# Local attention over spans of 64 keys, with tiles of 32 queries on TensorE

## The reference, cut to what matters

```
def local_attention(q, k, v):
    ...
    bk2, bv2 = (look(bk), look(bv))
    ...
    mask = (it < jb) | (it > jb + w) | (jb == -1)
    sim = jnp.einsum('bhwie,bhwje->bhwij', bq, bk2) * QK_SCALE
    sim = jnp.where(mask, -jnp.finfo(sim.dtype).max, sim)
    attn = jax.nn.softmax(sim, -1)
    out = jnp.einsum('bhwij,bhwje->bhwie', attn, bv2)
```

## Time and profile before

| what | us |
|---|---|
| median of three runs | 1869.86 |
| the profiled execution | 1866.89 |
| its span, first to last instruction | 1865.1 |
| TensorE busy, 14256 matmuls | 1740.2 (93%) |
| VectorE busy | 1612.1 (86%) |
| ScalarE busy | 1560.1 (84%) |
| GpSimd busy | 1334.2 (72%) |

### The profile page before, as it was taken

One profiled execution on the slowest core, in us unless ns is written; L12 is line 12 of the kernel. 1 busy time (PEld: TensorE's weight loads), 2 busy tenths in 40 slices (PEclk: granted clock), 3 DMA queues, 4 the chain that ended last, 5 costly groups with the idle time before them and its releaser, 6 DMA issues.

```text
span 1865.1 us, 39680 instructions
## 1 busy us (share of the span) xinstructions
PE 1740.2 (93%) x14256; PEld 1364.5 (73%) x14256; DVE 1612.1 (86%) x3044; ACT 1560.1 (84%) x4889; POOL 1334.2 (72%) x1864
## 2 busy tenths in 40 slices
PE   6589999899999999999999999999999999999995
PEld 4367777677777777777777777777777777777774
DVE  5689898898998988988989989989899889899872
ACT  3289889889898898898898898988988988988882
POOL 3378777787776777877877868777777778777660
PEclk9599999999999999999999999999999999999998
DMA  3000010000010000000000001000001000000000
GB/s 112 2 1 4 2 45 4 1 17 1 8 46 2 4 17 1 8 9 38 4 1 17 4 5 45 4 1 17 4 5 46 4 1 15 1 8 4 1 4 26
DMA packets 24153, 25.37 MB, mean 14 GB/s; under 512 B 13795, under 2 KB 21654, under 8 KB 23190
## 3 DMA queue, kind: packets, MB, share of 16 engines
q1 hardware_dynamic: 23958, 22.83, 4.0%
HBM read 18.65 MB, written 1.05 MB: 11 GB/s over the span
## 4 chain that ended last, share of the span: by engine, by line
PE 65%; DVE 24%; ACT 8%; issue 2%; DMA 1%; POOL 0%; SPq 0%; POOLq 0%; DVEq 0%
PE ps L382 8%; PE ps L403 7%; PE ps L371 7%; PE ps L391 7%; PE ps L363 5%; PE ps L365 5%; PE ps L364 5%; PE ps L411 5%; DVE t L910 3%; PE ps L377 3%; DVE nmax L930 3%; DVE t L912 3%; PE ps L442 3%; DVE xh L970 3%; DVE ss L895 3%
## 5 line engine op out<-in xcount | busy, mean ns | idle before, releaser
L621 ACT ACTIVATE pr<-ps,nbias,rn 128x128 f32<-128x128 f32 x1536 | 683.8, 471 | 9.6 <-DVE nbias L934 9.3
L743 POOL TENSOR_TENSOR t<-t 128x512 f32<-128x512 f32 x384 | 487.1, 1279 | 251.5 <-DVE t L912 248.1
L768 POOL TENSOR_TENSOR pr<-pr,rsum 128x512 f32<-128x512 f32 x384 | 404.5, 1054 | 40.6 <-DVE rsum L941 40.6
L621 ACT ACTIVATION_READ_ACCUMULATOR pr<-ps,nbias,rn 128x1 f32 x1536 | 335.6, 218 | 0.0
L363 PE MATMUL ps<-w_hi,xt_hi 128*128 128x512 f32 x576 | 272.0, 472 | 9.3 <-DVE t L912 6.0
L910 DVE TENSOR_TENSOR t<-ps,rope 128x512 f32<-128x512 f32 x384 | 260.9, 679 | 14.4 <-ACT sq L585 12.9
L930 DVE TENSOR_REDUCE nmax<-ps 128x8 f32<-128x1024 f32 x192 | 233.7, 1217 | 41.6 <-PE ps L382 40.5
L912 DVE TENSOR_TENSOR t<-ps,rope 128x512 f32<-128x512 f32 x384 | 259.8, 676 | 0.0
L895 DVE TENSOR_REDUCE ss<-sq 128x8 f32<-128x512 f32 x384 | 250.4, 673 | 1.2 <-ACT sq L585 1.2
L627 ACT ACTIVATE pT<-ps 128x512 f32<-128x512 f32 x384 | 234.6, 612 | 16.5 <-PE ps L391 16.5
L585 ACT ACTIVATE sq<-ps 128x512 f32<-128x512 f32 x384 | 224.6, 603 | 28.1 <-PE ps L365 14.9
(11 more groups left out here) (124 smaller groups left out, 2934.5 us busy)
## 6 DMA issues: line engine op xcount, KB each, us to landing
wqkv<-wqkv_in SPq DMA_DIRECT2D x6, 1536.0 KB, 13.0
wo<-wo_in SPq DMA_DIRECT2D x6, 512.0 KB, 10.6
xsh<-xr SPq DMA_DIRECT2D x24, 127.0 KB
w<-w_in SPq DMA_DIRECT2D x6, 342.0 KB, 7.2
w<-w_in SPq DMA_DIRECT2D x6, 172.5 KB
x<-x_in SPq DMA_DIRECT2D x4, 256.0 KB, 3.9
out<-x SPq DMA_DIRECT2D x4, 256.0 KB, 3.0
ctx<-ctx_in SPq DMA_DIRECT2D x4, 240.0 KB, 3.6
```

What stands on the lines that cost most here:

```text
L621: i = A(pr[:, g, k, :], ps[:, S_BANK[odd], k * P:(k + 1) * P], ACT.Exp, bias=nbias[:, h2, odd, k:k + 1], scale=rn[:, par(u), h2, 0, h:h + ...
L743: G.tensor_tensor(t1[:, c, :], t1[:, c, :], t2[:, c, :], ALU.add).then_inc(qk_added[c], 1)
L768: G.tensor_tensor(w, w, rsum[:, g // 2, g % 2, :].unsqueeze(2).broadcast_to([P, 4, P]), ALU.mult).then_inc(pr_ready[g], 1)
```

## The change

Scores, exponentials and probabilities are kept for a span of 64 keys per 32 queries, as the reference's windows have them. For query groups 0 to 3 the span starts at key 0, 0, 32 and 64.

- `scores` is done for all 16 heads in one stage: 8 head pairs x 4 query groups x 2 heads = 64 matmuls of 64 rows, 32 stationary columns and 64 moving keys. The four groups write different 32 partitions, the two heads different banks, so eight array tiles are in use. One mask per bank.
- `row_max`, `clamp_norm`, `guess_norm` and `refine_norm` are done once per unit for 16 heads. `exps` still has 16 instructions, of 64 columns. A head pair's probabilities lie side by side in 128 columns, so `transpose_p` has 8 transposes and `copy_pT` 2 copies.
- After the transpose an even head's keys lie in partitions 0 to 63 and an odd head's in 64 to 127. `weigh_values` needs v at the same partitions: six slices per head pair group, some from v, some from `v_win`, which SyncE fills with four copies per unit (`shift_v`).
- The columns of Wv and rows of Wo are reordered on input. The load of wqkv is split in six. Lags, banks and the order in every `step` are new; copies of q and k are all on ScalarE, both copies of v on VectorE.

```diff
+SPAN = 64
+WINDOW_START = [0, 0, 32, 64]
+BLOCKS = H // 2
...
+            def shift_v(u, odd):
+                sp.wait_ge(v_ready[odd], u + 1)
+                if u >= 2:
+                    sp.wait_ge(o_ps, 4 * (u - 1))
+                p, r = par(u), slice(E * odd, E * odd + E)
+                starts = WINDOW_START[1:3] if odd else WINDOW_START[2:4]
+                for n, t in enumerate(starts):
+                    sp.dma_start(v_win[r, p, n, :], v[t:t + SPAN, p, odd, :]).then_inc(v_shifted[odd][p], 16)
+            def step(s):   # SyncE
...
+                run(s, 3, shift_v, 1)
+                run_layer(s, 2, load_wo, 1)
+                run_quad(s, 6, shift_tokens)
+                run(s, 1, shift_v, 0)
...
+            def scores(u):
...
+                for c in range(BLOCKS):
+                    for g in range(P // WIN):
+                        for odd in range(2):
+                            r, q = slice(E * odd, E * odd + E), slice(WIN * g, WIN * g + WIN)
+                            i = mm(ps[q, S_BANK[odd], c * SPAN:(c + 1) * SPAN], qT[r, par(u), c, q],
+                                   kT[r, par(u), c, WINDOW_START[g]:WINDOW_START[g] + SPAN],
+                                   start=False, stop=c == BLOCKS - 1, skip_group_check=True)
...
+            def weigh_values(u):
+                p = par(u)
+                for h2 in range(2):
+                    if h2 == 1:
+                        pe.wait_ge(pt_ready[h2], u + 1)
+                    pe.wait_ge(v_shifted[h2][p], 32 * (u // 2 + 1))
+                even = [(0, 2 * WIN, v[0:E, p, 0]), (2 * WIN, WIN, v_win[0:E, p, 0]), (3 * WIN, WIN, v_win[0:E, p, 1])]
+                odds = [(0, 2 * WIN, v_win[E:P, p, 0]), (2 * WIN, WIN, v_win[E:P, p, 1]), (3 * WIN, WIN, v[E:P, p, 1])]
+                for j in range(BLOCKS // 2):
+                    for n in range(3):
+                        for b in range(2):
+                            for odd in range(2):
+                                c = 2 * j + b
+                                q, m, window = (even, odds)[odd][n]
+                                i = mm(ps[E * b:E * b + E, O_BANK[odd], j * P + q:j * P + q + m], window[:, c * E:(c + 1) * E],
+                                       pT[E * odd:E * odd + E, c, q:q + m], start=True, stop=True)
...
+            def exps(u, g):
+                    c, h = 4 * h2 + k, 2 * k + odd
+                    i = A(pr[:, c, odd * SPAN:(odd + 1) * SPAN], ps[:, S_BANK[odd], c * SPAN:(c + 1) * SPAN], ACT.Exp,
...
+            def normalise_p(u, h2):
+                w = pr[:, 4 * h2:4 * h2 + 4].rearrange("p c (o w) -> p (c o) w", o=2)
```

More of the change, by code:

```diff
@@ L104, in build @@
     kT = sb("kT", [P, 2, 8, P])
[L105 to L111, removed]
+    v = sb("v", [P, 2, 2, 512])
+    v_win = sb("v_win", [P, 2, 2, 512])
+    nmax = sb("nmax", [P, 2, BLOCKS])
+    nbias = sb("nbias", [P, 2, BLOCKS])
+    psums = sb("psums", [P, H])
+    rsum = sb("rsum", [P, H])
+    pr = sb("pr", [P, BLOCKS, 2 * SPAN])
+    pT = sb("pT", [P, BLOCKS, P])
     oT = sb("oT", [P, 2, 8, P])
@@ L199, in run_input, with run_layer @@
             task((s - lag) // QUAD + NQ)
-    def at(s, lag, l):
-        return s - lag == l * B
+    def run_layer(s, lag, task, first=0, last=L):
+        if (s - lag) % B == 0 and first <= (s - lag) // B < last:
+            task((s - lag) // B)
     def par(u):
@@ L230, in _, with load_qkv @@
                     sp.dma_start(x1[:, s, :], x_d[s].rearrange("b t d -> t b d")).then_inc(ld_x[q + 1], 16)
-            def load_qkv(l):
+            def load_qkv(l, c):
+                w = slice(CHUNK_COLS[c], CHUNK_COLS[c] + 512)
                 if l >= 1:
-                    for c in range(6):
-                        sp.wait_ge(w_ready[c], l)
-                sp.dma_start(wqkv[:], wqkv_d[l]).then_inc(ld_qkv, 16)
+                    sp.wait_ge(w_ready[c], l)
+                sp.dma_start(wqkv[:, w], wqkv_d[l, :, w]).then_inc(ld_qkv[c], 16)
             def load_scales(l):
@@ L273, in _ @@
             sp.dma_start(vec[:], vec_d.rearrange("l p v -> p l v")).then_inc(ld_vec, 16)
[L274 to L287, removed]
+            for s in range(FIRST_STEP, LAST_STEP):
+                step(s)
             for q in range(NQ):
@@ L372, in transpose_qk @@
                 i.then_inc(tq_ps[c], 1)
-            def scores(u, h2):
+            def scores(u):
+                for c in range(4):
+                    if c in (K0, K1):
+                        pe.wait_ge(tq_ready[c], u + 1)
                 for odd in range(2):
-                    mm(ps[:, S_BANK[odd], :], ident16[:], band16[:].rearrange("p a k -> p (a k)"), start=True, stop=False,
+                    mm(ps[:, S_BANK[odd], :], ident16[:], band16[:].rearrange("p c w -> p (c w)"), start=True, stop=False,
@@ L378, in scores @@
                        skip_group_check=True)
-                for k in range(4):
[L380 to L405, removed]
+                for c in range(BLOCKS):
[5 more added lines that the diff above has]
+                                   start=False, stop=c == BLOCKS - 1, skip_group_check=True)
+                            if c == BLOCKS - 1:
+                                i.then_inc(s_ps, 1)
@@ L454, in step @@
[L454 to L461, removed]
+                    bank_free_of_quad(s, f_h, 9, FCH, -2)
+                    project(s - 0, Q0)
+                if due(s, 8):
+                    ffn_transpose((s - 8) // QUAD)
@@ L484, in step @@
[L484 to L489, removed]
+                    scores(s - 1)
+                if live(s, 2):
+                    bank_free(s, (pt_ready[0], 2), (tq_ready[K0], 1))
+                    transpose_p(s - 2, 1)
@@ L532, in _ @@
+                if live(s, 2):
+                    bank_free_of_input(s, 14)
+                    bank_free_of_quad(s, x_final, 11, 1, NQ)
+                    weigh_values(s - 2)
             pe.wait_ge(ld_const, 80)
@@ L784, in step @@
-                run(s, 1, normalise_p, 0)
-                run(s, 1, lower_w, V1)
-                run(s, 0, normalise_k, 1)
-                run_quad(s, 6, copy_half)
-                for l in range(L):
-                    if at(s, 5, l):
-                        split_w1(l)
+                run(s, 0, rotate, Q1)
+                run_layer(s, 7, split_w1)
             pool.wait_ge(exponent_ready, 1)
@@ L954, in add_residual, with copy_o @@
+            def copy_o(u, odd):
+                dve.wait_ge(o_ps, 4 * u + 4)
+                V.tensor_copy(oT[:, par(u), 4 * odd:4 * odd + 4, :].rearrange("p a t -> p (a t)"), ps[:, O_BANK[odd], :]).then_inc(o_ready[odd], 1)
             def add_residual(u):
@@ new lines, in step @@
+                run(s, 2, row_max)
+                run_quad(s, 8, ffn_normalise)
+                run_quad(s, 10, ffn_gated, 1)
+                run_quad(s, 11, ffn_gated, 2)
+                run(s, 1, sum_squares, Q1)
+                run(s, 1, clamp_norm)
+                run(s, 1, copy_v, 0)
+                run(s, 1, copy_v, 1)
+                run(s, 3, copy_o, 1)
+                run_quad(s, 9, ffn_gated, 0)
+                run_quad(s, 7, ffn_stats)
+                run_quad(s, 8, ffn_affine)
@@ L1028, in step @@
-                run_input(s, 14, lower_xt)
-                run_quad(s, 8, ffn_gated, 2)
-                run_quad(s, 7, ffn_lower)
-                run_quad(s, 11, ffn_residual)
-                run(s, 0, copy_qk, K0)
-                run(s, 0, copy_qk, Q1)
-                for l in range(1, L):
-                    if at(s, -8, l):
-                        rope_tables(l)
+                run_layer(s, -8, rope_tables, 1)
             cross_stats_x(0)
```

449 lines of the change are left out of this document (221 added, 228 removed).

## The result

| what | us |
|---|---|
| median before, runs of the same chips | 1869.57 (1866.22 to 1872.99) |
| median after | 1895.61 (1892.82 to 1905.79) |
| ratio | 1.0149 (95%: 1.0107 to 1.0191) |
| profiled execution after, its span | 1895.38, 1893.6 |

The account below looks back on a forecast made before the run. TensorE was taken as the bound: 17.96 - 1.98 (less PE work) + 0.2 (v-copy waits) = 16.2 us a unit; 95 x 1.78 = 169 us off 1866.9 gave 1698, forecast as 1700 us, range 1640 to 1760 (chance 0.50).

Parts of the forecast that it names:

- PE's terms: TensorE per unit: mask 0.52, transposes 0.82, scores 2.1, values 1.5; sum 4.94 us against 6.92.
- rival 4: TensorE: full tile concurrency and a faster feed, PE 15.0 us a unit, 1595 us in all; chance 0.10.
- Rivals 1 and 2: TensorE: never more than two tiles at once, 1960 us, chance 0.13; or 15 ns an instruction, 1907 us, chance 0.11.
- the 9.3 of the forecast: TensorE's sequencer feed: 9.3 ns an instruction, giving scores 2.1 us and values 1.5 us.
- The Trainium skill's floor: TensorE: matmul starts never below about 25 ns apart; scores plus values would be 6.0 us; chance counted with rival 2.
- the paragraph on SyncE and the moved v: SyncE's queue: four v copies, at most 2.7 us of issue; PE waits 0.9 us every fourth step, 0.2 a unit.
- a falling clock as a sign of error: TensorE: a granted clock under 0.95 in the steady part, from thinner stages, would show the forecast wrong.
- rival 3: v copies or the scores-to-transpose_p chain set the step: weigh_values waits 1 us every step, 1775 us (1750 to 1860); chance 0.14.
- rival 2: TensorE: each instruction costs 15 ns, not 9; PE 0.4 us a unit more than now, 1907 us; chance 0.11.
- 96 x 1.98: TensorE's work: 1.98 us less per unit, from 6.92 to 4.94 us.
- 96 x 0.2: TensorE's new waits for v copies: 0.2 us a unit, bounds 0 and 2 us.
- 1.87: TensorE's idle time per period of four sequences: 1.87 us, taken as unchanged by the change.

Follow-up runs that it names:

- the first experiment: Against the kernel after: SyncE issues both v copies of unit s-1 before load_wo and shift_tokens, nothing else changed; 1749.72 us, ratio 0.9361 to the kernel before.
- the tile-by-tile kernel: On top of the first experiment: the same 64 score calls, all eight head pairs of one array tile in a row; 2088.13 us, ratio 1.1184.

## Why the prediction was wrong

**What held, by its own steps.** PE's terms were right or too high. In the first experiment's kernel the score stage took 1.41 us in the median (2.1 forecast), the value stage 1.53 at its shortest and 1.66 in the median, small waits inside included (1.5), the mask pair 0.53 (0.52). PE's busy time per unit is 60.09/4 = 15.02 us in the undisturbed kernel, a shade below the about 15.5 that the forecast implies and just the 15.0 of rival 4 (all tiles at once, a faster feed). Rivals 1 and 2 are refuted for this order: 256 instructions in 1.41 us are 5.5 ns each, neither 15 nor the 9.3 of the forecast.

The Trainium skill's floor ("TensorE: Matmul & The Clock Gate", Part 1, some 25 ns from one matmul's start to the next) is not borne out either: 11 ns here, where neighbours go to different tiles. Beside the chip's own rows, the rule would have been the wrong reason to expect a slower kernel.

Exponentials follow each other every 0.38 us (0.39), and the shortest steps of the periods shown take 14.8 and 14.9 us (14). VectorE gave 2.0 us a unit (196/96), not 2.6: the one product of the maxima for 16 heads takes 776 ns where the two for 8 took 321 each, so it costs 0.13 us where I had it save 0.3. GpSimd gave 2.8 (3.0), ScalarE 2.0 (1.9).

**The step that failed** is the paragraph on SyncE and the moved v: "I cost it at 0 in three steps and 0.9 us in the fourth". Its place was right, its mechanism half. It named the odd copy behind the even copy and xsh, before `weigh_values`, once in four steps. It took 0.68 us for every issue. The issue right behind xsh takes 6.9 us, the odd copy lands 3.1 us after its own issue, and PE stands 5.60 us in the step shown. Over the run the 23 such waits are 4.4 us on average (0.8 to 7.0), five times the 0.9. A second wait, behind the load of w2 (five times, 11 us in all), was not in the forecast. PE in the kernel after, across the wait:

```profile
1061.58 0.40 PE L469 MATMUL ps<-xhT_lo,w_hi 128*114 128x512 f32 x1
1067.57 0.34 PE L438 MATMUL ps<-pT,v 64*64 64x64 f32 x1 [5.60 <-DMA v_win<-v]
...
1071.73 0.63 PE L386 MATMUL ps<-w_hi,xt_hi 128*128 128x512 f32 x1
1072.16 0.63 PE L387 MATMUL ps<-w_lo,xt_hi 128*128 128x512 f32 x1
...
1073.77 0.39 PE L388 MATMUL ps<-w_hi,xt_lo 128*128 128x512 f32 x1
1074.00 0.39 PE L386 MATMUL ps<-w_hi,xt_hi 128*128 128x512 f32 x1
```

The second price is the clock. Busy time by stretch while PE waits (read as above; busy us of PE and loads are 0.00):

```profile
1062.40:1064.30 1.90, 0.00 (x0) 0.00 (x0) 1.79 (x4) 1.42 (x7) 0.41 (x1) 1.00 0.51 140
1064.30:1067.50 3.20, 0.00 (x0) 0.00 (x0) 0.09 (x1) 0.23 (x2) 0.00 (x0) 0.74 0.57 171
```

The granted clock falls while PE is idle. After the wait a matmul of 512 columns starts every 0.43 us (1.2 GHz), and only from about 1073 us every 0.23 (2.4 GHz); the value stage takes 2.78 us in place of 1.53. Per period that is the 44.9/24 = 1.9 us of busy time that the first experiment gives back. The forecast named a falling clock as a sign of error but priced it nowhere.

This is rival 3 with its price mis-sized. It was put at 1750 to 1860, from a wait of 1 us in every step; the wait was 4.4 us on average in one of four, and with the clock and the waits behind w2 it cost 146 us. That the result lies near rival 2's 1907 is chance: nothing of rival 2 was found.

**What is left without the wait.** The first experiment stands at 1749.72, 50 us over the forecast, though PE works less than forecast. Against the kernel before PE's busy time fell by 1740.2 - 1512.4 = 228 us, where 96 x 1.98 = 190 was forecast; its idle time grew by 110 us (124.9 to 234.6), where 96 x 0.2 = 19 was. That the time falls into the forecast's range is thus in part two errors against each other: PE's work fell by 38 us more than forecast, and 91 us of idle time were not foreseen. In the period shown PE idles 66.36 - 60.09 = 6.27 us, and the forecast took 1.87 as unchanged. Two sources are in the trace, and neither was isolated by a run:

- PE is no longer far ahead of the others. In the step from 946.96 ScalarE is busy for 16.64 of 18.26 us, in that from 995.45 VectorE for 16.57 of 17.87, and PE idles 2.1 us in each. ScalarE's share of the chain is 32% in this kernel, 8% in the kernel before. The forecast spread each engine's work evenly over four steps; the FFN work makes one step ScalarE's and another VectorE's.
- In score and value stages PE stops, as it seems for want of instructions. PE in the first experiment's kernel, one stage:

```profile
920.69 1.41 PE L409 MATMUL ps<-kT,qT 64*32 64x64 f32 x121
923.54 0.31 PE L409 MATMUL ps<-kT,qT 64*32 64x64 f32 x7 [1.44 <-issue]
```

The stage is cut after 121 of 128 matmuls and takes 3.09 us (923.78 - 920.69). PE's waits of this kind before score matmuls (us, times, longest, in this kernel):

```profile
PE ps L409 <- issue: 17.6, 12, 1.9
```

With the value stages there are 17 such gaps over 0.5 us, 21.5 us together, in that kernel (two of them just ahead of a value stage), and none in the kernel before. The page has 227 packets of the instruction queue for this kernel and 115 before, and 16 of the 17 gaps end 1.3 to 1.6 us after such a packet has landed. In the tile-by-tile kernel, whose score stages run the same instructions at a quarter of the pace, no score stage has such a gap. That it is instruction fetch is read from these times and from that one contrast; no run changed the fetch alone.

How the rest of the 91 us of idle time divides, beyond these 21.5, stays open.

## What to carry to other kernels

Before placing a new DMA on a queue, list the issue times of everything already there, least and most, and look at the instruction behind each slow transfer of many short rows: a hold may be in the trace of before and cost nothing only because nobody waits for its victim. Then order the queue by deadline; here four calls in another order were worth 146 us and turned 1.5% slower into 6.4% faster. A wait of some microseconds on TensorE costs its length and, as here, a stretch at half clock behind it, and an estimate of a pipeline whose engines lie within 2 us of each other has to be made step by step, not from the mean of a period.

## What the runs showed of the hardware

- A DMA of 508 rows of 256 bytes (127 partitions) went at 15 to 18 GB/s, at most two rows at a time, and held the next DMA of its queue for 6.9 us. In four DMAs of 127 rows the first held its neighbour little (0.9 us in the median), the last ones some 2.0 each. 64 rows of 2 KB held nothing. With the 508 rows on ScalarE's queue, DMAs on SyncE's were not held.
- The same transfer issued by GpSimd cost that engine 4.64 us and landed after 18.5 us, against 0.73 us to issue on SyncE's queue.
- With neighbours on different tiles 128 fp32 matmuls of 64 columns start in 1.41 us (11 ns each), with neighbours on the same tile in 5.91 us (46 ns).
- At this pace (5.5 ns an instruction) TensorE stops in its score and value stages for 0.5 to 1.9 us now and then, 17 times in 1747 us; 16 of these gaps end 1.3 to 1.6 us after a packet of the instruction queue has landed.
- The granted clock fell from full to half while TensorE waited; with a mean of 0.938 in place of 0.971 the same matmuls were busy 45 us longer.
